# Selective scan in a four-layer vision block: GpSimd makes the input product in three of twelve steps and not in four

## The reference, cut to what matters

```python
def selective_scan(xs, dts, As, Bs, Cs, Dsk):
    ...
    def step(h, inp):
        u_t, d_t, B_t, C_t = inp
        dA = jnp.exp(d_t[..., None] * As)
        h = h * dA + (d_t * u_t)[..., None] * B_t[:, :, None, :]
        y = jnp.einsum('bkcn,bkn->bkc', h, C_t)
        return (h, y)
...
out_y = selective_scan(xs, dts, As, Bs, Cs, Ds.reshape(K, DI))
```

## Time and profile before

| what | value |
|---|---|
| median of 3 runs | 5550.74 us (5530.37 to 5564.74) |
| the profiled execution | 5553.52 us |
| its span | 5551.7 us, 75892 instructions |
| mean granted TensorE clock | 0.793 |
| PE busy | 4176.4 us (75%) |
| DVE busy | 3814.9 us (69%) |
| ACT busy | 2729.8 us (49%) |
| POOL busy | 1752.5 us (32%) |

### The profile page before, as it was taken

How to read it: one execution, slowest core, us unless ns; L and a number is a source line. 1 busy time by engine, 2 the same in 40 slices (tenths; PEclk the granted TensorE clock), 3 DMA queues, 4 the chain that set the end, 5 groups by cost and what they waited for, 6 DMA issues and landing times. The chain is left out here.

```text
span 5551.7 us, 75892 instructions
## 1 busy us (share of the span) xinstructions
PE 4176.4 (75%) x23106; PEld 1514.5 (27%) x23106; DVE 3814.9 (69%) x5359; ACT 2729.8 (49%) x3579; POOL 1752.5 (32%) x989
## 2 busy tenths in 40 slices
PE   5587883642888885644588876676999999999997
PEld 3344441210111112211111112352333333333332
DVE  4355553455888884556688896556877877877874
ACT  1254550564444443366344444232666666666663
POOL 0000000144999982044699996000000000000000
PEclk9798996655667667755576678775999999999998
DMA  3311113123222222023222223033111111111112
GB/s 108 90 21 28 27 23 62 41 77 105 56 61 55 64 55 56 22 66 91 76 61 59 57 61 77 11 127 93 57 46 43 42 43 43 45 43 43 42 43 76
DMA packets 152578, 318.15 MB, mean 57 GB/s; under 512 B 36922, under 2 KB 95299, under 8 KB 148206
## 3 DMA queue, kind: packets, MB, share of 16 engines
q1 hardware_dynamic: 152174, 313.01, 21.0%
HBM read 204.44 MB, written 108.02 MB: 56 GB/s over the span
## 5 line engine op out<-in xcount | busy, mean ns | idle before, releaser
L1874 DVE TENSOR_REDUCE l3a_mx<-l3a_mx 128x1 f32<-128x384 f32 x2719 | 1326.1, 550 | 352.7 <-PE l3a_mx L1744 327.5
L1849 ACT ACTIVATE l3a_p<-l3a_s 128x1024 f32<-128x1024 f32 (+1 forms) x1080 | 978.1, 936 | 428.4 <-PE l3a_s L1765 414.4
L1264 POOL TENSOR_TENSOR l_scan_sc<-l_scan_s,l_scan_repc 128x768 f32<-128x768 f32 x576 | 1036.5, 1809 | 125.3 <-DVE l_scan_s L1242 116.1
L1744 PE MATMUL l3a_mx<-l3a_k,l3a_q 124*128 124x384 f16 x2719 | 868.1, 340 | 23.0 <-issue 18.4
L1201 ACT ACTIVATE l_scan_da<-l_scan_da,l_scan_a 128x768 f32<-128x768 f32 x576 | 504.1, 875 | 736.1 <-PE l_scan_da L1125 734.3
L1765 PE MATMUL l3a_s<-l3a_q,l3a_k 125*128 125x512 f16 (+1 forms) x2160 | 751.8, 362 | 29.2 <-issue 28.0
L1125 PE MATMUL l_scan_da<-l_scan_dt,l_scan_pick 96*128 96x512 bf16 (+1 forms) x1152 | 400.9, 443 | 261.5 <-DVE l_scan_s L1242 260.8
L1783 PE MATMUL l3a_o<-l3a_p,l3a_vh 128*32 128x512 f32 (+1 forms) x4332 | 592.6, 565 | 0.0
L1712 POOL TENSOR_TENSOR l3a_norm<-l3a_out,l3a_spread 128x512 f32<-128x512 f32 x25 | 32.2, 1288 | 1626.4 <-DMA l3a_spread<-l_inverses 1626.4
L1152 PE MATMUL l_scan_y<-l_scan_sc,l_scan_sum 128*32 128x256 f32 x3456 | 518.7, 541 | 1.4 <-POOL l_scan_sc L1264 1.4
L1125 PE MATMUL l_scan_dup<-l_scan_du,l_scan_pick 96*128 96x512 bf16 (+1 forms) x1152 | 382.3, 424 | 159.3 <-DMA l_scan_dt<-l_dtp 136.2
(11 more groups left out here) (194 smaller groups left out, 5249.5 us busy)
## 6 DMA issues: line engine op xcount, KB each, us to landing
l3a_q<-l_qx SPq DMA_DIRECT2D x104, 486.0 KB
l_dup<-l_prep_parts_u SPq DMA_DIRECT2D x16, 1296.0 KB, 6.2
l_dtp<-l_prep_parts_t SPq DMA_DIRECT2D x16, 1296.0 KB, 8.3
l_scan_du<-l_dup SPq DMA_DIRECT2D x144, 144.0 KB
l_scan_dt<-l_dtp SPq DMA_DIRECT2D x144, 144.0 KB
l_scan_repb<-l_bcp SPq DMA_DIRECT2D x48, 384.0 KB
l_scan_repc<-l_bcp SPq DMA_DIRECT2D x48, 384.0 KB
l3a_q<-l_hx SPq DMA_DIRECT2D x104, 72.0 KB
```

Source lines behind the costliest of these rows:

```text
L1264: pool.tensor_tensor(SC[:, st % NSC, :], S[:, n, :], REPC[k % 2][:], ALU.mult).then_inc(weighted, 1)
L1744: pe.matmul(out[:, 0:RG], Q[h % HPB][0:rows, variant(g), qt * 128:(qt + 1) * 128], K[h % HPB][0:rows, g * RG:(g + 1) * RG], start=True, st ...
L1849: act.activation(P[:, g % NP, :, 0:w], s_ps[n % 2][:, :, 0:w], ACT.Exp).then_inc(exped, 1)
L1874: dve.tensor_reduce(MX[:, h % HPB, qt, g:g + 1], mx_ps[bank][:, 0:RG], AX_X, ALU.max)\
```

## The change

In the function `ssm_scan` the steps whose input product GpSimd makes are no longer every third one. Of the twelve steps of a chunk they are 2, 5 and 8; step 11 becomes VectorE's. ScalarE's copy of its restored input goes with it. Both layers use the function.

Two lists give the steps of either engine over the whole layer, and every count that was a formula of st is now a lookup in one of them. At a GpSimd step TensorE and ScalarE restore and copy the input of the next GpSimd step, so at step 8 of a chunk that of step 2 of the next chunk (number 14). GpSimd makes the input product of step 14 behind the state product of step 6; before, it stood behind that of step 9. VectorE makes the product of step 11 between the scans of steps 9 and 10. The buffers' counts stay as they are.

```diff
@@ -1012,11 +1012,10 @@
     PASSES = 2 * B * 2
     CHUNKS = PASSES * NC
     STEPS = CHUNKS * NN
-    TRIPLES = STEPS // NT
     PIECE = TC // NT
     NSC = 9
     LAG = 8
-    GP = NT - 1
+    ON_POOL = (2, 5, 8)
     with Scope(nc, name) as s:
         PICK = s.sb("pick", [DI, NG, 128], BF16)
         SUM = s.sb("sum", [128, NG, 32])
@@ -1046,11 +1045,17 @@
             s.sem(n) for n in ("scanned", "weighted", "piece_summed", "y_taken", "y_stored"))
         BANKS = [(0, CH), (CH, TC - CH)]

-        order = [GP]
+        on_pool = [st for st in range(STEPS) if st % NN in ON_POOL]
+        on_dve = [st for st in range(STEPS) if st % NN not in ON_POOL]
+        pool_nth = {st: n for n, st in enumerate(on_pool)}
+        dve_nth = {st: n for n, st in enumerate(on_dve)}
+
+        order = [on_pool[0]]
         for st in range(STEPS):
-            nxt = st if st % NT != GP else st + NT
-            if nxt < STEPS:
-                order.append(nxt)
+            if st in dve_nth:
+                order.append(st)
+            elif pool_nth[st] + 1 < len(on_pool):
+                order.append(on_pool[pool_nth[st] + 1])
         nth_du = {st: n for n, st in enumerate(order)}

         def place(st):
@@ -1066,10 +1071,6 @@
         def way(ap, d):

             return ap[:, ::-1] if d else ap
-
-        def dve_steps_before(st):
-
-            return st // NT * (NT - 1) + st % NT

         with s.block() as block:
             @block.sync
@@ -1093,8 +1094,8 @@
                               .then_inc(loaded[i], 16)
                     if k >= 2:
                         sp.wait_ge(weighted, (k - 1) * NN)
-                        sp.wait_ge(pool_multiplied, (k - 1) * NG)
-                        sp.wait_ge(multiplied, (k - 1) * NG * (NT - 1))
+                        sp.wait_ge(pool_multiplied, (k - 1) * len(ON_POOL))
+                        sp.wait_ge(multiplied, (k - 1) * (NN - len(ON_POOL)))
                     for j, dst in enumerate((REPB, REPC)):
                         sp.dma_start(dst[i][:], bc_dram[2 * p + j, :, span(c)].unsqueeze(0).to_broadcast([8, NS, TC]))\
                           .then_inc(rep_loaded[i], 16)
@@ -1132,10 +1133,10 @@
                     pe.wait_ge(loaded[k % 2], (k // 2 + 1) * 96)
                     if m >= 1:
                         before = order[m - 1]
-                        if before % NT == GP:
-                            pe.wait_ge(du_copied, before // NT + 1)
+                        if before in pool_nth:
+                            pe.wait_ge(du_copied, pool_nth[before] + 1)
                         else:
-                            pe.wait_ge(multiplied, dve_steps_before(before) + 1)
+                            pe.wait_ge(multiplied, dve_nth[before] + 1)
                     restore(st, DU, du_ps, du_made)

                 def sum_piece(tr, k):
@@ -1158,12 +1159,13 @@
                                            YF[:, c * TC + k * PIECE:c * TC + (k + 1) * PIECE], start=False, stop=k != 0)
                     mm.then_inc(piece_summed, 1)

-                restore_du(GP)
+                restore_du(on_pool[0])
                 for st in range(STEPS + LAG):
                     if st < STEPS:
-                        nxt = st if st % NT != GP else st + NT
-                        if nxt < STEPS:
-                            restore_du(nxt)
+                        if st in dve_nth:
+                            restore_du(st)
+                        elif pool_nth[st] + 1 < len(on_pool):
+                            restore_du(on_pool[pool_nth[st] + 1])
                         if st >= 2:
                             pe.wait_ge(scanned, st - 1)
                         restore(st, DT, da_ps[st % 2], dt_made)
@@ -1185,17 +1187,17 @@
                     act.activation((YS if d else YF)[:, span(c)], y_ps[:, 0:TC], ACT.Copy).then_inc(y_taken, 1)

                 def copy_du(st):
-                    tr = st // NT
+                    tr = pool_nth[st]
                     act.wait_ge(du_made, nth_du[st] + 1)
                     if tr >= 2:
                         act.wait_ge(pool_multiplied, tr - 1)
                     act.activation(DUS[:, tr % 2, :], du_ps[:, 0:TC], ACT.Copy).then_inc(du_copied, 1)

-                copy_du(GP)
+                copy_du(on_pool[0])
                 for st in range(STEPS):
                     k, p, d, c, n = place(st)
-                    if st % NT == GP and st + NT < STEPS:
-                        copy_du(st + NT)
+                    if st in pool_nth and pool_nth[st] + 1 < len(on_pool):
+                        copy_du(on_pool[pool_nth[st] + 1])
                     column = p % 4 * NN + n
                     act.wait_ge(dt_made, st + 1)
                     act.activation(da_ps[st % 2][:, 0:TC], da_ps[st % 2][:, 0:TC], ACT.Exp,
@@ -1213,25 +1215,24 @@

                 def weigh_inputs(st):
                     k, p, d, c, n = place(st)
-                    m = dve_steps_before(st)
+                    m = dve_nth[st]
                     dve.wait_ge(rep_loaded[k % 2], (k // 2 + 1) * 32)
                     if m >= 3:
-                        used = m - 3
-                        dve.wait_ge(scanned, used // (NT - 1) * NT + used % (NT - 1) + 1)
+                        dve.wait_ge(scanned, on_dve[m - 3] + 1)
                     dve.wait_ge(du_made, nth_du[st] + 1)
                     dve.tensor_tensor(BU[:, m % 3, :], du_ps[:, 0:TC], REPB[k % 2][:], ALU.mult).then_inc(multiplied, 1)

                 weigh_inputs(0)
                 for st in range(STEPS):
                     k, p, d, c, n = place(st)
-                    if st + 1 < STEPS and (st + 1) % NT != GP:
+                    if st + 1 in dve_nth:
                         weigh_inputs(st + 1)
-                    if st % NT == GP:
-                        dve.wait_ge(pool_multiplied, st // NT + 1)
-                        bu = BUP[:, st // NT % 2, :]
+                    if st in pool_nth:
+                        dve.wait_ge(pool_multiplied, pool_nth[st] + 1)
+                        bu = BUP[:, pool_nth[st] % 2, :]
                     else:
-                        dve.wait_ge(multiplied, dve_steps_before(st) + 1)
-                        bu = BU[:, dve_steps_before(st) % 3, :]
+                        dve.wait_ge(multiplied, dve_nth[st] + 1)
+                        bu = BU[:, dve_nth[st] % 3, :]
                     dve.wait_ge(exped, st + 1)
                     if st >= NN:
                         dve.wait_ge(weighted, st - NN + 1)
@@ -1247,23 +1248,23 @@
             def _(pool):
                 def weigh_inputs(st):
                     k = st // NN
-                    tr = st // NT
+                    tr = pool_nth[st]
                     pool.wait_ge(rep_loaded[k % 2], (k // 2 + 1) * 32)
                     pool.wait_ge(du_copied, tr + 1)
                     if tr >= 2:
-                        pool.wait_ge(scanned, (tr - 2) * NT + GP + 1)
+                        pool.wait_ge(scanned, on_pool[tr - 2] + 1)
                     pool.tensor_tensor(BUP[:, tr % 2, :], DUS[:, tr % 2, :], REPB[k % 2][:], ALU.mult)\
                         .then_inc(pool_multiplied, 1)

-                weigh_inputs(GP)
+                weigh_inputs(on_pool[0])
                 for st in range(STEPS):
                     k, p, d, c, n = place(st)
                     pool.wait_ge(scanned, st + 1)
                     if st >= NSC:
                         pool.wait_ge(piece_summed, ((st - NSC) // NT + 1) * NT)
                     pool.tensor_tensor(SC[:, st % NSC, :], S[:, n, :], REPC[k % 2][:], ALU.mult).then_inc(weighted, 1)
-                    if st % NT == 0 and st + NT + GP < STEPS:
-                        weigh_inputs(st + NT + GP)
+                    if st + 2 in pool_nth and pool_nth[st + 2] + 1 < len(on_pool):
+                        weigh_inputs(on_pool[pool_nth[st + 2] + 1])


 def ssm_gate(nc, name, t, pre, eye, ones_mean, y_dram, skip_dram, z_dram, YG):
```

## The result

| kernel | median of its runs | ratio to before (95% interval) |
|---|---|---|
| before | 5543.01 us (9 runs) | 1 |
| changed | 5566.61 us (9 runs) | 1.0041 (1.0026 to 1.0057) |

The change costs about 23 us (14 to 32 by the interval). The sum had said +11 us, so the cost is twice the sum. That the median nevertheless lies within 5 us of the forecast 5562 us is in part luck: the sum was added to the median of three runs, 5550.74 us, and nine runs of the same kernel give 5543.01. The single profiled execution of the changed kernel took 5564.1 us, 10.6 us above that of before. This pair alone would mislead: from the first product to the end of the last scan the two stages grew by 26.7 us (749.8 and 739.3 us before, 756.7 and 759.1 after), and the stages around them, which are the same code, happened to be 16 us shorter.

The account below looks back on a forecast made before the run. Neither VectorE nor GpSimd was full over a stage; TensorE's low-clock chain made VectorE wait. +10.3 + 4.8 - 4.1 = +11.0 us on the profiled 5553.52 gives 5564.5; the median lies 2.8 lower, so 5562 us, range 5534 to 5592.

Parts of the forecast that it names:

- The sum: Whole kernel: the predicted terms added up, +10.3 + 4.8 - 4.1 = +11.0 us.
- TensorE's chain: Both scans, low clock: TensorE restores the next input late, behind decay and sum, so VectorE idles 1.06 us per triple.
- VectorE's product: Step 11 of each chunk: 48 added products of 0.85 us, 40.8 us uncovered; idle before opening products leaves +10.3 us.
- The longer chain: Low-clock chunk ends: step 12's decay waits for step 10's scan, losing 0.21 us in 23 chunks, +4.8 us.
- GpSimd's relief: Both scans: 86.8 us less GpSimd work gives back a quarter of the sums' 16.4 us of waits, -4.1 us.
- Rival B: Both scans: GpSimd was the bound, all 16.4 us of waits go, -9.7 us, 5541 us; chance 0.22.
- the clock rival: TensorE's clock moves: all low +51.8 us, 5603 us, chance 0.05; all high -122.7 us, 5428 us, chance 0.05.
- ScalarE's copy: 48 fewer copies of a restored input, 38.9 us less on ScalarE; covered, worth nothing.
- the transfers: GpSimd's product for step 14 needs the next chunk's B earlier; margin some 8 us, so no cost.
- Rival A: Last triple of every chunk: the product is not covered, VectorE decides, +40.8 us, 5592 us; chance 0.18.
- The clock rule: Skill's advice on TensorE: matmuls without long gaps keep the clock up; then no idle, product costs full 40.8 us.
- My checks: Scans: both stages within 10 us of 750 and 739; idle before products down about 30 us; GpSimd idles more.

Follow-up runs that it names:

- the move of one call: Kernel before, with TensorE restoring the next input behind the decay and ahead of the sum's piece (also called the moved kernel): 5420.9 us, ratio 0.9767.
- relief alone: Kernel before, with GpSimd's input product of step 11 one column wide and not 768: 5553.4 us, ratio 1.0002.
- the kernel with the narrow product: Changed kernel, with VectorE's product of step 11 one column wide, the new order kept: 5547.3 us, ratio 1.0000.
- the load: Changed kernel with the next input restored ahead of the sum, plus one unread GpSimd product where step 11's was: 5457.5 us, ratio 0.9833.

## Why the prediction was right, point by point

*That TensorE's chain sets VectorE's pace*: right at the low clock, shown by the move of one call, which took 129 us off and left the product without a wait there.

*VectorE's product, 40.8 us less the covered part, +10.3*: the mechanism was right, the size a little low. The cover came as said: of the 35.6 us of idle in front of the opening products 2.7 are left, and 2.5 stand in front of step 11's product, whose short wait lies in the same gap. Unrounded, 30.3 us went, where the step said 30.5. But the product costs 0.90 us of VectorE's busy time and not 0.85, 43.0 in all, so 12.7 us are left and not 10.3.

*The longer chain, +4.8*: right. The predicted 0.21 us shows as the step from 2.59 to 2.85, and the idle in front of step 13's product grew by 5.3 us.

*GpSimd's relief, -4.1*: the term that failed. Its bound of 16.4 us was a misreading: 15.1 of it are idle time of the weight loader, and the matmuls of the sums waited 1.4 us for GpSimd's products in both scans together. Even the waits as counted did not follow GpSimd's load: 16.4 us before, 19.0 with the change, 13.5 with relief alone. Relief alone measured 1.0002, which leaves room for 0 to -7 us but shows no gain. Rival B's -16.4 rests on the same row. With this term at 0 and the others as measured, 43.0 - 30.3 + 5.3 = 18.0 us.

*What is left* is 5 us to the median, and 9 us to the 26.7 by which the two scans grew in this pair of traces. The traces show 7 us of it as more idle in front of other products: 5.2 before steps 3, 6 and 9 and 2.0 before step 7, which the sum does not have. They stand in a stage whose clock fell from 0.72 to 0.66, and that lies in the direction of the clock rival, at a small part of its price. The clock did fall with the change: over whole executions it is 0.787 on the mean of the nine changed runs and 0.792 over the 49 runs of the kernel before that stood beside the experiments. But the kernel with the narrow product has 0.789 on the mean of twelve runs and an unchanged time, which speaks against the clock alone costing 20 us. What it costs here was not isolated.

*ScalarE's copy and the transfers at nothing*: nothing contradicts it. No wait of GpSimd for B shows but the first of each scan.

*Rival A, uncovered, +41*: excluded in this kernel by 1.0041 (its upper end is 32 us) and found where it was said to hold, once the idle is gone (+37 for the load). *Rival B, -10*: excluded by the interval and by relief alone. *The clock rule* of the Trainium skill, "TensorE: Matmul & The Clock Gate", section "Why this matters for your kernels", would have left no idle to cover the product. The trace after disagrees again: waits of 1.06 us recur at the low clock, 0.50, though TensorE is busy 633 of 756 us in the first scan and waits 1.2 us for a scan at the longest.

*My checks*: the second scan grew by 20 us, not within 10; the waits fell by 17.7 us and not 30, as others grew; the rest held. One reading of the rows was off besides: I took GpSimd's chunk at 16 x 1.808 = 28.93 us, but its instructions start 1.77 us apart where none waits (1609.97 to 1611.74 above), which makes 28.3, less than VectorE's 28.73. So rival B's 0.20 us in each uncovered chunk had no ground.

## What to carry to other kernels

An instruction moved to a busier engine costs, in the main, what the idle time at its new place does not cover, so look at that place step by step, not at busy shares: the same product cost 10, 23 or 34 us by its place in the chunk. Relief of an engine that follows others turns into its idle time. Idle time of the weight loader is not a wait of the matmuls, so look which of the two a row counts. And an idle time that recurs with one releaser is worth more than any balance of loads around it: taking the sum out of the chain gave 129 us, and the kernel before with that move, at 5420.9 us, is the fastest of those that leave nothing out.

## What the hardware showed that I had not expected

The moved kernel beat the bound that I had worked out for it, 28.93 us per chunk: its scan takes 676 us for 24 chunks, 28.2 each. GpSimd's product at 1609.97 lasts 1.83 us, and the next starts 1.77 us behind its start, so instructions in a row overlap a little. At that pace 16 products make 28.3 us.

And TensorE's granted clock rose from 0.68 and 0.72 to 0.82 in both scans when its order changed, with the same matmuls and a smaller busy share (530 of 676 us against 619 of 750). The clock has two levels, so the two scans spent about 894 us at the low one before and 487 after the move. An estimate from these numbers: at the old rate of waits, 163.4 us in 894, the 487 us would hold 89 us, and 34 were measured. By it, some 55 us of waits went because the chain is shorter, and some 74 may have gone because the clock was up. Why the clock rose, the runs do not show.
